# GNN and mixture-of-experts kernel on one core: one-hot selections for two groups of edges in two VectorE operations, and fewer waits on PE

## The reference

```python
def gcn(x, src, dst, ew, W, b):                 # 12500 x 256, 200000 edges sorted by dst
    xW = x @ W
    deg = segment_sum(ew, dst) + 1.0
    dinv = rsqrt(deg)
    norm = dinv[src] * ew * dinv[dst]
    agg = segment_sum(norm[:, None] * xW[src], dst) + (dinv * dinv)[:, None] * xW
    return agg + b
x = x + relu(gcn2(relu(gcn1(layernorm(x)))))
t = layernorm(x)
p = softmax(t @ router_w.T); rw, re = top_k(p, 2); rw /= rw.sum()
x = x + t + sum over 8 experts e of combine[:, e] * (gelu(t @ w1[e] + b1[e]) @ w2[e] + b2[e])
```

## Time and profile before

| | before |
|---|---|
| median of three runs | 5221.11 us (5214.46 to 5225.19) |
| profiled execution | 5177.12 us |
| its span | 5175.3 us |
| PE busy | 3841.7 us (74%), 27222 matmul instructions |
| PE weight loads busy | 3496.5 us (68%) |
| VectorE busy | 2298.3 us (44%), 8827 instructions |
| ScalarE busy | 722.4 us (14%) |
| POOL busy | 3003.7 us (58%) |
| selections (L1047) | 3136 instructions, 838.6 us busy |
| gathers (L461) | 3136 instructions, 2968.1 us busy |

### The profile page before, as it was taken

One profiled execution on the slowest core, in us unless ns is written; L12 is line 12 of the kernel. 1 busy time (PEld: TensorE's weight loads), 2 busy tenths in 40 slices (PEclk: granted clock), 3 DMA queues, 4 the chain that ended last, 5 costly groups with the idle time before them and its releaser, 6 DMA issues.

```text
span 5175.3 us, 82233 instructions
## 1 busy us (share of the span) xinstructions
PE 3841.7 (74%) x27222; PEld 3496.5 (68%) x27223; DVE 2298.3 (44%) x8827; ACT 722.4 (14%) x2277; POOL 3003.7 (58%) x3241
## 2 busy tenths in 40 slices
PE   3445565555555555555558999999999999999999
PEld 3424454554555545555557899889989899988998
DVE  6732222222222222222224655566556655656655
ACT  1020000000000000000001222222222222222222
POOL 0104666666666666666666666666666666656663
PEclk9998766766666666667668999999999999999999
DMA  3244333333333333333333333333333333333332
GB/s 95 62 144 122 99 97 97 100 96 98 98 97 100 96 97 99 95 98 98 97 94 93 95 97 99 96 96 96 96 98 96 96 97 98 96 93 95 95 97 59
DMA packets 243540, 500.39 MB, mean 97 GB/s; under 512 B 61453, under 2 KB 141656, under 8 KB 243179
## 3 DMA queue, kind: packets, MB, share of 16 engines
q0 software_dynamic: 150528, 411.24, 28.0%
q1 hardware_dynamic: 87210, 79.56, 4.9%
q10 hardware_dynamic: 5440, 5.01, 0.3%
HBM read 456.90 MB, written 38.67 MB: 96 GB/s over the span
## 4 chain that ended last, share of the span: by engine, by line
PE 28%; DVE 19%; POOL 18%; issue 16%; another core or an unknown queue 14%; DMA 3%; DVEq 2%; SPq 1%; ACT 0%; POOLq 0%; ACTq 0%
POOL msg L461 18%; PE part L736 11%; DVE sel L1047 5%; PE psY L730 5%; PE psH L721 3%; PE psY L736 3%; DVE mix L1175 2%; PE psH L736 2%; DMA msg<-ytab,srcT 1%; DVEq L272 1%; DVE accbuf L1055 1%; DVE accbuf L989 1%; DVE nt L1129 1%; PE psT L689 1%
## 5 line engine op out<-in xcount | busy, mean ns | idle before, releaser
L461 POOL DMA_INDIRECT msg<-ytab,srcT x3136 | 2968.1, 946 | 1878.2 <-issue 962.3
L736 PE MATMUL part<-sel,msg 128*128 128x96 f32 x8384 | 1155.9, 293 | 255.6 <-issue 207.9
L736 PEld LDWEIGHTS part<-sel,msg 128*128 128x128 f32 x8384 | 1113.6, 210 | 310.6 <-issue 270.1
L730 PE MATMUL psY<-w_s,hS 128*128 128x256 f32 x3136 | 838.1, 390 | 19.6 <-DVE mix L1175 10.1
L1047 DVE TENSOR_SCALAR sel<-iota,relT,ewT 128x96 f32<-128x96 f32 x3136 | 838.6, 342 | 2.5 <-ACT accbuf L514 1.6
L721 PEld LDWEIGHTS psH<-tokS,w_s 128*128 128x128 f32 x6272 | 811.3, 192 | 36.1 <-issue 0.5
L721 PE MATMUL psH<-tokS,w_s 128*128 128x128 f32 x6272 | 813.9, 275 | 0.4 <-issue 0.4
L1055 DVE TENSOR_TENSOR accbuf<-accbuf,part 128x192 f32 x524 | 185.6, 354 | 1215.8 <-remote 744.3
L553 ACT ACTIVATE hS<-psH,b_s 128x128 f32<-128x128 f32 x1568 | 487.7, 362 | 1411.9 <-PE psH L721 798.6
L730 PEld LDWEIGHTS psY<-w_s,hS 128*128 128x128 f32 x3136 | 543.3, 191 | 113.7 <-issue 64.3
L736 PE MATMUL psH<-sel,msg 128*128 128x96 f32 x2080 | 370.0, 335 | 251.4 <-issue 232.6
(11 more groups left out here) (167 smaller groups left out, 2024.8 us busy)
## 6 DMA issues: line engine op xcount, KB each, us to landing
msg<-ytab,srcT POOLq DMA_INDIRECT x3136
msg<-in_x SPq DMA_DIRECT2D x194, 128.0 KB, 2.1
ytab<-xS SPq DMA_DIRECT2D x99, 128.0 KB, 15.2
ytab<-msg SPq DMA_DIRECT2D x98, 128.0 KB, 1.7
xS<-in_x SPq DMA_DIRECT2D x98, 128.0 KB
out<-res SPq DMA_DIRECT2D x98, 128.0 KB
w_s<-in_L_ffn_w ACTq DMA_DIRECT2D x2, 2048.0 KB
accbuf<-in_dst SPq DMA_DIRECT2D x1, 588.0 KB
```

Of the source, the lines that this page charges most:

```text
L461: pool.indirect_dma_start(msg[:, r * GT + j, :], None, ytab[l], bass.IndirectOffsetOnAxis(ap=srcT[:, g * GT + j:g * GT + j + 1].bitcast(U3 ...
L730: mm = pe.matmul(psY[e % 2][:, 0:D], hS[:, e % 2, m, :], w2_s[:, e, m, :], start=(m == 0), stop=(m == KD - 1))
L736: m = pe.matmul(slot[:, h * W:(h + 1) * W], msg[:, tile0 + j, h * P:(h + 1) * P], sel[:, sel0 + j, :], start=(j == 0), stop=(j == GT - 1))
```

## The change

One call of `selection` now makes the selections of two groups, eight tiles: an is_equal of 8 x 96 columns (iota and the relative targets, both by broadcast), and then, behind a wait for its own signal, a multiplication in place by the weights. Each of the two signals s_sel once, so the count after a pair is the same as before. As the groups of a pair run backwards through the edges, the pair's tiles lie in sel in the order of the edges, and PE reads the slot r ^ 1. The calls move: VectorE selects after the add of every odd group, for the pair that begins three groups later, and no longer after even groups. PE waits for a pair's s_sel value at its first group. In layer 0 an odd group waits for nothing of its own; `sums` of layer 0 no longer waits for linD, and `turn_y2` no longer for y2C.

```diff
         def sums(l, s, biases_behind=1):
             pe.wait_ge(s_agg[l], s.k)
-            wait(pe, s_linD[l], s.k - 1)
             if l == 1:
+                wait(pe, s_linD[l], s.k - 1)
                 wait(pe, s_bias, s.k - biases_behind)
...
         def turn_y2(s):
             pe.wait_ge(s_y2, s.k)
-            wait(pe, s_y2C, s.k - 1)
...
-            if l == 0 and n % 2 == 0:
-                pe.wait_ge(s_msg[(q + 1) % MR], ((q + 1) // MR + 1) * (16 * GT))
-            pe.wait_ge(s_msg[m], (q // MR + 1) * (16 * GT))
-            pe.wait_ge(s_sel, q + 1)
+            if l == 1 or n % 2 == 0:
+                if l == 0:
+                    pe.wait_ge(s_msg[(q + 1) % MR], ((q + 1) // MR + 1) * (16 * GT))
+                pe.wait_ge(s_msg[m], (q // MR + 1) * (16 * GT))
+                pe.wait_ge(s_sel, q // 2 * 2 + 2)
             if l == 1:
                 pe.wait_ge(s_added, q - 1)
-            products(sums_of(l, n), m * GT, r * GT).then_inc(s_part, 1)
+            products(sums_of(l, n), m * GT, (r ^ 1) * GT).then_inc(s_part, 1)
...
         def selection(q):
             g, r = NG - 1 - q % NG, q % R
-            wait(v, s_part, q - R + 1)
-            for j in range(GT):
-                t = v.tensor_scalar(sel[:, r * GT + j, :], iota[:, 0:W], relT[:, g * GT + j:g * GT + j + 1],
-                                    ewT[:, g * GT + j:g * GT + j + 1], ALU.is_equal, ALU.mult)
-            t.then_inc(s_sel, 1)
+            tiles = slice((g - 1) * GT, (g + 1) * GT)
+            to = sel[:, r * GT:(r + 2) * GT, :]
+            wait(v, s_part, q - R + 2)
+            v.tensor_tensor(to, iota[:, 0:W].unsqueeze(1).broadcast_to([P, 2 * GT, W]),
+                            relT[:, tiles].unsqueeze(2).broadcast_to([P, 2 * GT, W]), ALU.is_equal).then_inc(s_sel, 1)
+            v.wait_ge(s_sel, q + 1)
+            v.tensor_tensor(to, to, ewT[:, tiles].unsqueeze(2).broadcast_to([P, 2 * GT, W]), ALU.mult).then_inc(s_sel, 1)
...
-                if q + R < NG:
-                    selection(q + R)
+                if r % 2 and q + R < NG:
+                    selection(q - 1 + R)
...
-                    if q + R < 2 * NG:
-                        selection(q + R)
+                    if r % 2 and q + R < 2 * NG:
+                        selection(q - 1 + R)
```

More of the change, by code:

```diff
@@ L1208, in _ @@
         v.wait_ge(s_y1C, NB + XS)
-        for r in range(R):
+        for r in range(0, R, 2):
             selection(r)
```

## The result

The kernel before took 5217.78 us (median of 4, 5214.46 to 5225.19), the change **5300.89 us** (5298.38 to 5302.36): ratio **1.0154**, 95% interval 1.0142 to 1.0166, +83.1 us. The forecast was 5309.

The account below looks back on a forecast made before the run. It took layer 0 to be nearest bound by POOL's gathers and layer 1 by a ring through VectorE, PE and POOL. 98 iterations x 0.90 us = 88 us, all in layer 1, on the median 5221.1 gave 5309 us, range 5215 to 5332.

Parts of the forecast that it names:

- The pair's price: VectorE's two 768-column selection operations: 945 ns each, 1.84 to 1.93 us together, about what eight small ones cost.
- Turn(1), +0.90 us, ring 25.7 us: Layer 1: the pair lengthens turn(1), between share(2) and tok, by 0.90 us; iteration 25.7 us, 88 us in all.
- the ring: Layer 1's 24.84 us iteration: share(2) to tok's end 4.59, to POOL's next gather 2.53, gathers until next share(2) 17.72.
- the signs named for it: Layer 1: share(2)'s idle time 2.8 us, PE's wait for tok about 1.7, POOL's pause before group 2 about 2.9.
- share(2) waits for PE's signal all the same: Layer 1: turn(0) loses 0.95 us, but share(2) starts no sooner; its idle time grows from 1.83 to 2.8 us.
- In the ring nothing gives it back: Layer 1: no other piece of the iteration shrinks to offset turn(1)'s +0.89 to +0.98 us; POOL's pause only grows.
- The rival of slack: Layer 1: share(2)'s release moves forward by turn(0)'s 0.95 us and pays for the 0.90: no change, 5221 us; chance 0.10.
- Layer 0, nothing: Layer 0: moved selections and dropped PE waits cost or gain nothing; POOL's pauses stay about 3.1 us, iterations 23 us.
- the 10 us allowed: Layer 0: the forecast counts as wrong if this layer moves by over 10 us.
- The two operations shut POOL out: Layer 0: operations with two SBUF inputs delay gathers, 1.9 us per iteration, 186 us in all, 5495 us; chance 0.05.
- the gather of 3508.68 with the residual inside: Layer 1: evidence against POOL being shut out; a two-SBUF-input residual started inside this gather, which took its usual 0.95 us.
- PE's fewer waits: Four dropped per layer 0 iteration: worth nothing; rival, chance 0.13, gave 5172 us for two or 5035 for all four.

Follow-up runs that it names:

- before_third: The kernel before, unedited, run again on chip D for a trace: 5218.22 us, ratio 1.0007.
- e3: The change with each pair's selections made by eight one-tile operations instead of two large ones, chip A: 5213.48 us, 1.0073 of the kernel before.
- e6: The kernel before with layer 1's one-tile selections made in pairs in turn(0) and turn(2), chip B: 4755.46 us, ratio 0.9998.
- e8: The kernel before with layer 1's one-tile selections in pairs in turn(0) and turn(2), again, chip C: 4754.54 us, ratio 0.9998.
- e9: The kernel before with layer 1's one-tile selections in pairs in turn(0) and turn(2), a third time, chip D: 5243.99 us, ratio 1.0046.
- after_again: The whole change, unedited, run again on chip B: 4890.37 us, 1.0276 of the kernel before.
- e4: The kernel before with each group's selection made by two 384-column operations at the old places, chip B: 4799.22 us, ratio 1.009.
- e5: The change with layer 1's pair selections moved to turn(0) and turn(2), chip B: 4841.44 us, 1.0176 of the kernel before.
- e2: The kernel before with only the change's fewer PE waits, chip A: 5173.8 us, ratio 0.9997.
- e1: The change with PE's old waits put back, chip A: 5220.95 us, 1.0084 of the kernel before.

## Why the prediction was right, and where not

- *The pair's price* (945 ns each, 1.84 to 1.93 us): 953 and 958 ns, 1.86 us. Right.
- *Turn(1), +0.90 us, ring 25.7 us:* the piece grew by 0.90. The iteration grew by 0.86 on the chip of the result, so 98 x 0.90 = 88 came close to 83, and over all iterations the rest of the ring kept its length there (20.30 us, 20.34 in before_third). But the signs named for it came out smaller: 1.40 us of idle time before share(2) and not 2.8, 1.39 for PE's wait and not 1.7, 2.30 for POOL's pause and not 2.9. As a law it is wrong, and that the number came so close is in part luck. Two sentences failed: "share(2) waits for PE's signal all the same", and "In the ring nothing gives it back". With the places alone share(2) came earlier and most was given back (e3: 0.38 us of time for 0.90). On chips B and C, where PE has no idle time in layer 1 with the places of e6 and e8, the change's places cost 0.53 to 0.58. And made shorter, the piece gave nothing (e9). I had one timeline in which a path was tight, and took from it that it was the only one. The rival of slack, 0.10, was half true (e3).
- *Layer 0, nothing:* right there within the 10 us allowed (+3.2 at its end), by two things that nearly cancel. Gathers got longer (POOL busy +81 us between 440 and 2680 us), while its pauses shrank. In the kernel before on chip D, then in the change, 600 to 2400 us:
```profile
POOL msg L461 <- remote: 264.2, 85, 3.4
```
```profile
POOL msg L461 <- remote: 191.4, 67, 4.3
```
  That is 73 us less over 1800. Where POOL has no such pause the longer gathers are paid in full: on chip B the gathers of layer 0 take 87 us more in after_again than in e6 (1573.8 against 1487.2), and layer 0 84; in e4 they take 43 more (1529.7), and layer 0 39.
- *The two operations shut POOL out* (0.05): its mechanism is real, but it was priced at 186 us in layer 1. Where the runs isolate it, it costs 84 in layer 0 and nothing in layer 1 (e5). What I read against it, the gather of 3508.68 with the residual inside, was the wrong case: that gather had begun before the operation. It is the gather that **begins** inside one that is longer. The last section has the rule.
- *PE's fewer waits:* nothing (e2). Right for them alone.
- *What share of the result's 83 us is the kind's:* e3 and e1 differ by 7 us on chip A, 38 and 46, which is within what this kernel's times tell. On the result's chip the iteration is 0.9 us longer in place of 0.5, with two runs of gathers joined and the new wait for ScalarE. The joined runs alone aren't the cause: e1 has them too, with three pauses of POOL an iteration in place of four in 93 of 95, and takes 25.3 us. What e1 lacks is the wait for ScalarE, 8 times and 7.1 us between 2750 and 5100 against 85 times and 62.3. No run separates it from PE's fewer waits or the chip. That stays open.

No version was faster than the kernel before.

## What to carry to other kernels

A stretch without a gap ahead of a wait need not set the time: 0.9 us more in it cost 0.4 to 0.9 us here, and 0.95 us less gave nothing. What a change of it is worth depends on the next path, so look for the work that would be waited for then. Where VectorE operations with both inputs in SBUF replace one-input ones beside GpSimd gathers, look at how long the gathers become, and try shorter operations: here 768 columns at a time cost 84 us in layer 0 and 384 at a time 39. And look whether the trace of before has the time of the median: here the two lay 0.8% apart, half of the effect. Then ask the same of single iterations: three or five long ones made half of a mean's growth.

## What the runs showed of the hardware

**A gather that begins inside an operation with both inputs in SBUF ends 0.82 us after that operation.** POOL and VectorE in layer 0 of after_again and e4_kind_only:
```profile
1502.02 0.95 DVE L1052 TENSOR_TENSOR sel<-iota,relT 128x768 f32<-128x768 f32 x1
1502.41 1.38 POOL L461 DMA_INDIRECT msg<-ytab,srcT  x1 [0.30 <-issue]
...
1512.38 0.95 DVE L1052 TENSOR_TENSOR sel<-iota,relT 128x768 f32<-128x768 f32 x1
1512.85 1.30 POOL L461 DMA_INDIRECT msg<-ytab,srcT  x1 [0.30 <-issue]
```
```profile
1507.58 0.56 DVE L1051 TENSOR_TENSOR sel<-sel,ewT 128x384 f32<-128x384 f32 x1
1507.75 1.21 POOL L461 DMA_INDIRECT msg<-ytab,srcT  x1 [0.30 <-issue]
...
1518.11 0.95 POOL L461 DMA_INDIRECT msg<-ytab,srcT  x1 [0.30 <-issue]
1518.25 0.56 DVE L1051 TENSOR_TENSOR sel<-sel,ewT 128x384 f32<-128x384 f32 x1
```
1502.97 + 0.82 = 1503.79 = 1502.41 + 1.38; 1513.33 + 0.82 = 1514.15 = 1512.85 + 1.30; 1508.14 + 0.82 = 1508.96 = 1507.75 + 1.21; the last gather began first and takes its 0.95. In the change, 3506.66 + 1.65 = 3508.31 is 0.82 behind the multiplication of 3506.53 to 3507.49. Of the gathers that begin inside a selection's operation in the change, after_again and e4, 0.05 us or more after its start, 1304 of 1307 keep to this within 0.02 us; those that begin in the first 0.04 us take their usual 0.95 in 229 of 234 cases. The residual, whose inputs both lie in SBUF too, does the same to 90 gathers of the change; with one-input selections, in before_third, no gather takes over 1.09 us. A gather of 0.95 us is lengthened only if the operation has over 0.13 us left when it begins, and then by the rest; so an operation of half the columns costs less than half per piece: twice as many of them (e4) cost layer 0 39 us where the pairs cost 84. The Trainium skill (SBUF — State Buffer, Who interferes with whom) says that such an instruction contends with a GpSimd instruction that reads SBUF and that the order of issue decides who blocks. The rows agree for the gather that comes second; where the gather came first (1518.11), neither it nor the operation is longer (0.95 and 0.56 us). The same section tells of a probe in which tensor_tensor didn't stall a DMA, and infers that the making of descriptors needs only the write interface; here the gathers are slower by 71 ns on the mean, and no run separates their descriptors from their reading of the indices.

**PE's instructions come apart on some chips and not on others.** In layer 0 (600 to 2400 us), what PE waited for, in before_third (chip D) and in e6 (chip B):
```profile
PE psG L672 <- issue: 228.2, 163, 3.2
PE psY L736 <- issue: 167.8, 147, 2.5
PE psH L736 <- issue: 160.4, 141, 2.5
PE part L736 <- issue: 156.3, 125, 3.1
```
```profile
PE psH L736 <- DMA msg<-ytab,srcT: 220.3, 60, 6.1
PE part L736 <- DMA msg<-ytab,srcT: 217.4, 60, 6.2
PE psY L736 <- DMA msg<-ytab,srcT: 209.2, 60, 6.0
```
On D 713 us of 1800 are idle time ahead of single matmuls for nothing that the profile shows, and POOL has the pauses shown above (264.2 us), in which it waits for PE's products; on B PE waits for gathers alone, POOL has no pause over 0.3 us, and the same layer 0 ends 299 us sooner. This, more than any edit, sets the kernel's time: 4756 or 5217. I saw it in the earlier trace rows and took it as a constant of the chip. What holds PE back on chips A and D isn't shown, and some of this idle time can be waits that the profile doesn't name, as with tok in before_third. The granted clock between 600 and 2400 us is 0.69 on D and 0.75 on B, as a cause or as an effect, but from 2800 to 4600 it is 1.00 on both, and there, too, an iteration takes 25.04 against 23.58 us.
